# A decoder layer on one core: epsilon, the rotated sum and the last normalisation on GpSimd, the causal mask in quarters

## The chip, the cores and the metric

The kernel runs on one core of one Trainium2 chip. Its engines are TensorE (PE, with PEld for its weight loads), VectorE (DVE), ScalarE (ACT), GpSimd (POOL) and SyncE (SP, which only issues DMAs here). Each engine runs its own instructions in order and waits for semaphores that the others raise. The metric is the device time of one execution in microseconds (us), the median of several runs.

## What is computed

The reference is one decoder layer for 64 sequences of 64 rows with 256 features: rotary attention, a banded attention over context rows, a gated feed-forward layer with ternary weights, and a layer norm after each. Shortened:

```python
def _layernorm(x, g, b, eps=1e-05):
    mu = jnp.mean(x, axis=-1, keepdims=True)
    var = jnp.mean((x - mu) ** 2, axis=-1, keepdims=True)
    return (x - mu) * jax.lax.rsqrt(var + eps) * g + b
q = (_layernorm(x, qn_g, qn_b) @ Wq + bq)      # k, v likewise; 16 heads of 16
q = _rotary(q * scale, x)                      # a*fre - b*fim, a*fim + b*fre, by pairs
qn = _layernorm(q, ln_g, ln_b)                 # per head
scores = qn @ kn / sqrt(hd); scores = where(causal, scores, min)
out = softmax(scores) @ v @ Wo + bo
x = _layernorm(x + attn(x))
x = _layernorm(x + xattn(x, ctx))              # 8 heads of 8, |i - j| <= 64
# ffn: h = silu(gate) * up; hn = h * rsqrt(mean(h * h) + eps); hn @ w_proj
x = _layernorm(x + ffn(x))
```

## The kernel before

**Tiles and steps.** The 4096 rows are cut into 32 tiles of 128 rows (two sequences). The tiles run through a software pipeline that is written out by hand. Every engine has a function `step(at)`, called 41 times. In each step it does pieces of work of several tiles, and `at(-3)` is the tile that is three steps old. The order of the `put_...` calls inside `step` is the order on that engine. Nothing reorders it, so an instruction that waits holds up all that stands behind it. In the middle every step works on eight or nine tiles at different stages. The first six steps also hold the quantisation of the feed-forward weights (`quantise`, on DVE with ACT).

**Waits.** Each piece of work raises a semaphore of its own (`S["x2_lo"]` and so on). An instruction that reads what its own engine has just written waits for it too. On DVE `Chain` does that: it raises and waits after each instruction.

**The normalisations.** `put_x_stats`, `put_y1_stats`, `put_y2_stats` and `put_y3_stats` on DVE take mean and variance (`bn_stats`, `bn_aggr`) into `mv` and add epsilon into `base` (lines 1177, 1247, 1306, 1351). POOL raises `base` to the power -0.5 into `rstd` (`put_x_pow` and its like, lines 985, 1016, 1036, 1048), and DVE applies both. `put_yout` (line 1358, DVE) does so for the output, and `put_out` on SP stores it a step later. For the feed-forward layer ACT sums the squares (`put_sqsum`), DVE turns the sum into a mean plus epsilon (`put_hid_mean`, line 1332), POOL raises it to -0.5 (`put_hid_pow`, line 1044), ACT scales into `hsplit` (`put_h_hi`, line 842), and DVE computes the remainder in two halves (`put_h_lo`, line 1338). Behind `put_h_hi` ACT makes `headsT` (`put_ot`) and `attnT` (`put_aT`). PE transposes with line 559 what `put_h_hi` made, and its second group of line 492 waits for both `put_ot` and `put_aT`. The first group of line 492 stands ahead of line 559.

**Rotation.** POOL multiplies `qk` with sine and cosine into `rot2` and `rot1` (`put_rotated`, lines 993 and 994), the last work of its step. DVE adds the two (line 1201) and centres each head (lines 1202, 1203, `put_centred`). In the next step POOL goes on with `xbo` (line 1012), `x2_lo` (line 1040), `y3_pow` and the selects that cut the band (lines 1023, 1025). PE transposes `x2_hi` and `x2_lo` with line 518 and waits for `x2_lo` there.

**The mask.** `put_s_ps` on PE writes the causal mask (0 or -1e30, the same 64 rows twice) into two PSUM banks through an identity (line 360), two matmuls of 128 rows and 512 columns in bf16. On top of it the scores are summed with matmuls of 64 rows on the four quarters of the array (line 364).

Other lines: 430 the projections of the banded attention, 447 and 467 its scores for the maximum and for the exponential, 479 its values, 394 the values of the first attention (64 matmuls of 17 columns), 505 and 511 its output projections (511 waits for `gated` on POOL, line 1032), 1276 the row maxima, 1240 `y1`, 1187 `xn`, 1000 the powers of the head variances, 1007 `qkn`.

## Time and profile before

| | |
|---|---|
| runs | 1167.52, 1168.0, 1165.63 us, median 1167.52 |
| profiled execution | 1166.15 us, its span 1164.4 us |
| mean granted TensorE clock | 0.926 of full speed |
| busy in the span | PE 1050.6 us (90%), PEld 651.8 (56%), DVE 964.9 (83%), ACT 756.8 (65%), POOL 737.3 (63%) |
| chain that ended last | PE 73%, DVE 14%, POOL 4%, ACT 4%, issue 3%, DMA 1% |

A profile shows one execution. Busy time is the time in which an engine has an instruction in work; matmuls are pipelined, so a busy PE isn't PE at its peak. The chain follows the work that ended last back through what released it. In brackets behind an instruction stands how long its engine was idle before it, and whose signal ended that. PE's records are incomplete by a few per cent: line 360 has 33 rows for 64 matmuls.

### The profile page before, as it was taken

The numbers are of one execution on the slowest core, as the hardware profiler recorded it, in microseconds if no ns is written. First come the engines' busy times: TensorE is split into PE (matmuls) and PEld (weight loads), VectorE is DVE, ScalarE is ACT, GpSimd is POOL, SyncE is SP. The second block draws the span as 40 slices with busy tenths as digits, with TensorE's granted clock in tenths as the row PEclk, the third lists the DMA queues.
The fourth block names the chain that finished last, engine by engine and source line by source line (L and its number), as shares of the span: only waits on it lengthen the run. The fifth ranks groups of instructions, "written<-read, shape, count | busy, mean of one in ns | idle before, by whom it ended". The sixth has DMA issues, their size and how long they took to land.

```text
span 1164.4 us, 26192 instructions
## 1 busy us (share of the span) xinstructions
PE 1050.6 (90%) x10393; PEld 651.8 (56%) x10456; DVE 964.9 (83%) x2049; ACT 756.8 (65%) x1209; POOL 737.3 (63%) x1034
## 2 busy tenths in 40 slices
PE   4265899999999999999999999999999999999775
PEld 2143555666666666556655666666566556665442
DVE  5759778888898998998999899899989998887633
ACT  2343367677776777766777777777767777776652
POOL 1534477776677667767666677667767666664431
PEclk8656799999999999999999999999999999999877
DMA  6000000000000000000000000000000000000000
GB/s 213 10 5 10 16 15 16 16 11 11 20 21 20 21 20 20 21 20 21 2 19 21 20 21 20 21 20 21 21 20 21 3 19 20 17 16 11 10 20 9
DMA packets 26889, 25.04 MB, mean 22 GB/s; under 512 B 6160, under 2 KB 26000, under 8 KB 26768
## 3 DMA queue, kind: packets, MB, share of 16 engines
q1 hardware_dynamic: 24368, 20.23, 6.0%
q10 hardware_dynamic: 2400, 3.15, 0.8%
q8 instruction: 83, 1.36, 0.5%
q14 instruction: 38, 0.31, 0.1%
HBM read 14.19 MB, written 4.19 MB: 16 GB/s over the span
## 4 chain that ended last, share of the span: by engine, by line
PE 73%; DVE 14%; POOL 4%; ACT 4%; issue 3%; DMA 1%; SPq 0%; POOLq 0%; DVEq 0%
PE ps L430 10%; PE ps L479 8%; PE ps L394 6%; PE ps L333 5%; PE ps L548 5%; PE ps L565 5%; PE ps L532 5%; PE ps L447 4%; PE ps L467 4%; DVE hsplit L1338 3%; PE ps L340 3%; PE ps L364 3%; PE ps L378 2%; DVE rowmax L1276 2%; PE ps L511 2%
## 5 line engine op out<-in xcount | busy, mean ns | idle before, releaser
L1023 POOL TENSOR_SCALAR_AFFINE_SELECT prob<-prob 128x256 f32<-128x256 f32 (+1 forms) x256 | 137.5, 537 | 201.2 <-ACT prob L805 201.1
L1276 DVE TENSOR_REDUCE rowmax<-ps 128x4 f32<-128x768 f32 x256 | 243.2, 950 | 16.5 <-PE ps L447 15.7
L805 ACT ACTIVATE prob<-ps 128x768 f32<-128x768 f32 x256 | 207.0, 809 | 53.7 <-PE ps L467 53.3
L1000 POOL TENSOR_TENSOR hsum<-hsum,minus_half 128x8 f32<-128x8 f32 x128 | 210.7, 1687 | 36.6 <-DVE hsum L1211 33.4
L796 ACT ACTIVATE high<-ps,bx_col 128x512 f16<-128x512 f32 x128 | 99.6, 778 | 94.7 <-PE ps L430 91.9
L430 PE MATMUL ps<-x,wx_qk 128*128 128x256 f32 x512 | 139.9, 407 | 9.1 <-DVE k_rows L1264 4.4
L1025 POOL TENSOR_SCALAR_AFFINE_SELECT prob<-prob 128x512 f32<-128x512 f32 (+1 forms) x256 | 135.0, 527 | 0.0
L479 PE MATMUL ps<-prob,v_pad 128*32 128x192 f32 x2048 | 111.8, 336 | 1.0 <-POOL prob L1025 1.0
L430 PEld LDWEIGHTS ps<-x,wx_qk 128*128 128x128 f32 x512 | 93.0, 197 | 31.5 <-issue 13.7
L447 PE MATMUL ps<-k_rows,q_rows 24*128 24x192 f16 x1024 | 89.3, 254 | 4.0 <-DVE rowmax L1276 3.7
L467 PE MATMUL ps<-q_rows,k_rows 26*128 26x192 f16 x1024 | 88.2, 251 | 2.2 <-ACT prob L805 2.1
L1032 POOL TENSOR_TENSOR gated<-zr,enc 128x256 f32<-128x256 f32 x32 | 23.3, 729 | 97.1 <-ACT zr L819 97.1
L849 ACT ACTIVATE hT<-ps 128x1024 f16<-128x1024 f16 x64 | 65.6, 1025 | 19.3 <-PE ps L559 17.2
L394 PE MATMUL ps<-v_own,probT_a 64*64 64x17 f32 x1024 | 73.8, 212 | 4.1 <-ACT probT_a L781 4.1
L447 PEld LDWEIGHTS ps<-k_rows,q_rows 24*128 24x128 f16 x1024 | 29.1, 93 | 84.8 <-issue 69.8
L479 PEld LDWEIGHTS ps<-prob,v_pad 128*32 128x32 f32 x2048 | 53.9, 110 | 40.0 <-issue 16.9
L394 PE MATMUL ps<-v_swap,probT_a 64*64 64x17 f32 x1024 | 73.8, 212 | 2.1
L394 PEld LDWEIGHTS ps<-v_own,probT_a 64*64 64x64 f32 x1024 | 67.5, 140 | 9.3 <-issue 9.3
L394 PEld LDWEIGHTS ps<-v_swap,probT_a 64*64 64x64 f32 x1024 | 67.4, 140 | 5.3 <-PE ps L394 5.3
L333 PE MATMUL ps<-wqkv,xnT 128*128 128x512 f32 x128 | 67.8, 655 | 0.5 <-ACT xnT L757 0.5
L993 POOL TENSOR_TENSOR rot<-qk,sinT 128x256 f32<-128x256 f32 x64 | 46.1, 743 | 34.5 <-DVE qk L1191 34.5
L565 PE MATMUL ps<-wproj,hT 128*128 128x256 bf16 x512 | 66.2, 286 | 1.1 <-ACT hT L849 1.1
(147 smaller groups left out, 2440.7 us busy)
## 6 DMA issues: line engine op xcount, KB each, us to landing
v_swap<-v_own SPq DMA_DIRECT2D x64, 68.0 KB, 2.1
xin<-in_x SPq DMA_DIRECT2D x32, 128.0 KB, 2.1
enc<-in_ctx SPq DMA_DIRECT2D x32, 128.0 KB, 2.2
out<-yout SPq DMA_DIRECT2D x32, 128.0 KB, 2.0
prob<-in_w_gu ACTq DMA_DIRECT2D x4, 512.0 KB, 8.6
prob<-in_w_proj ACTq DMA_DIRECT2D x2, 512.0 KB, 13.0
q_rows<-negmax SPq DMA_DIRECT2D x64, 8.0 KB
q_rows<-in_Wkv SPq DMA_DIRECT2D x1, 512.0 KB, 7.8
```

The lines of the kernel that those rows point to most:

```text
L333: last = mm(ps[:, G6, :], xnT[:, i, :], wqkv[:, i, 0:512], start=i == 0, stop=i == 1)
L394: last = mm(ps[64 * b:64 * b + 64, G6, col:col + 17], probT_a[64 * half:64 * half + 64, slot // 2, 64 * b:64 * b + 64], vals[64 * half:64 ...
L430: last = mm(ps[:, (G7, G5, G5, G5)[c], XT * n:XT * n + XT], wx_qk[:, c, n, :], x1[:, t.x1_buf, :], start=True, stop=True)
L447: last = mm(ps[:, MXB + j, at:at + QW], q_rows[q, t.buf, ng, own], k_rows[q, t.buf, ng, others], start=True, stop=True)
L467: last = mm(ps[:, STB + j, at:at + QW], k_rows[q, t.buf, ng, own], q_rows[q, t.buf, ng, others], start=True, stop=True)
L479: last = mm(out[:, cols[kb]], v_pad[:, t.buf, kb, 4 * c + hq, :], prob[:, 4 * c + hq, kb, :], start=kb == 0, stop=kb == 1, skip_group_chec ...
L565: last = mm(ps[:, G6, 0:256], hT[:, i // 8, i % 8, :], wproj[:, i % 8, :], start=i == 0, stop=i == 15)
L805: copy(prob[:, 2 * c:2 * c + 2, :, :].rearrange("p u a b -> p u (a b)"), ps[:, STB:STB + 2, 0:2 * QW], ACT.Exp, scale=float(XD) ** -0.5).t ...
L1000: last = g.tensor_tensor(hsum[:, 1, h], hsum[:, 0, h], minus_half[:, h], ALU.pow)
L1023: g.affine_select(out=lead, in_=lead, compare_op=ALU.is_ge, fill=0.0, base=BAND - 64 * kb, pattern=[[0, 4], [1, cut]], channel_multiplier=-1)
L1025: last = g.affine_select(out=trail, in_=trail, compare_op=ALU.is_ge, fill=0.0, base=BAND + 64 * kb - cut, pattern=[[0, 4], [-1, QW - cut]] ...
L1276: v.tensor_reduce(of_head[:, hq:hq + 2, 2 * ng:2 * ng + 2], ps[:, MXB:MXB + 2, 0:2 * QW].rearrange("p j (a b) -> p j a b", a=2), AX, ALU.m ...
```

## The change

On POOL the four epsilon adds now stand right in front of the powers, each with a semaphore of its own that POOL waits for. The sum of squares gets its factor 1/1024 inside ACT's square (scale 1/32), and POOL adds epsilon to it, so that DVE's `put_hid_mean` is gone and `hid_pow` waits for `sqsum` on ACT. The add of the rotated parts moves from DVE to POOL, and `put_yout` moves from DVE to POOL, between the first two powers of the heads and `put_hid_pow`. The mask matmuls are four of 64 rows on the four quarters. `put_x_stats` signals after its last instruction. Everything else keeps its order.

```diff
@@ put_s_ps, PE
                 for r in range(2):
-                    mm(ps[:, G6 + r, :], identb[:, :], causal[:, :], start=True, stop=False, skip_group_check=True)
+                    q = slice(64 * r, 64 * r + 64)
+                    for b in range(2):
+                        mm(ps[64 * b:64 * b + 64, G6 + r, :], identb[q, q], causal[q, :], start=True, stop=False,
+                           skip_group_check=True, tile_position=(64 * r, 64 * b))
@@ put_sqsum, ACT
-                copy(sq_junk[:, :], hid[:, :], ACT.Square, accum_out=hss[:, 0:1]).then_inc(S["sqsum"], 1)
+                copy(sq_junk[:, :], hid[:, :], ACT.Square, scale=1.0 / 32, accum_out=hss[:, 0:1]).then_inc(S["sqsum"], 1)
@@ put_x_pow, POOL (put_y1_pow, put_y2_pow, put_y3_pow likewise)
                 pool.wait_ge(S["x_stats"], t.at(1, 1))
+                g.tensor_scalar(base[:, 0, :], mv[:, 0, 1:2], EPS, None, ALU.add).then_inc(S["eps0"], 1)
+                pool.wait_ge(S["eps0"], t.at(1, 1))
                 g.tensor_tensor(rstd[:, 0, :], base[:, 0, :], expo[:, :], ALU.pow).then_inc(S["x_pow"], 1)
@@ put_rotated, POOL
-                g.tensor_tensor(heads3(rot1[:, :]), heads3(qk[:, :]), cos_b, ALU.mult).then_inc(S["rotated"], 1)
+                g.tensor_tensor(heads3(rot1[:, :]), heads3(qk[:, :]), cos_b, ALU.mult).then_inc(S["rotated_c"], 1)
+                pool.wait_ge(S["rotated_c"], t.at(1, 1))
+                g.tensor_tensor(rot2[:, :], rot1[:, :], rot2[:, :], ALU.add).then_inc(S["rotated"], 1)
@@ put_hid_pow, put_yout, POOL
-                pool.wait_ge(S["hid_mean"], t.at(1, 1))
+                pool.wait_ge(S["sqsum"], t.at(1, 1))
+                g.tensor_scalar(hss[:, 2:3], hss[:, 0:1], 4 * RMS_EPS, None, ALU.add).then_inc(S["eps_hid"], 1)
+                pool.wait_ge(S["eps_hid"], t.at(1, 1))
                 g.tensor_tensor(hss[:, 3:4], hss[:, 2:3], expo[:, :], ALU.pow).then_inc(S["hid_pow"], 1)
...
+            def put_yout(t):
+                pool.wait_ge(S["y3_pow"], t.at(1, 1))
+                if t.has(3):
+                    pool.wait_ge(s_out[t.back(3).buf], t.back(3).dma(1))
+                g.tensor_scalar(yout[:, t.buf, :], y3[:, :], mv[:, 3, 0:1], rstd[:, 3, 0:1], ALU.subtract, ALU.mult).then_inc(S["yout"], 1)
@@ step, POOL
                     put_head_pow(t, 0)
                     put_head_pow(t, 1)
+                t = at(-8)
+                if t:
+                    put_yout(t)
                 t = at(-7)
                 if t:
                     put_hid_pow(t)
@@ put_x_stats, DVE
-                v.tensor_scalar(base[:, 0, :], mv[:, 0, 1:2], EPS, None, ALU.add).then_inc(S["x_stats"], 1)
                 chain(v.scalar_tensor_tensor(rot[:, 0:1], mv[:, 0, 0:1], mv[:, 0, 0:1], mv[:, 0, 1:2], ALU.mult, ALU.add))
-                chain(v.reciprocal(rot[:, 1:2], rot[:, 0:1]))
+                v.reciprocal(rot[:, 1:2], rot[:, 0:1]).then_inc(S["x_stats"], 1)
@@ put_centred, DVE
-                chain(v.tensor_tensor(rot2[:, :], rot1[:, :], rot2[:, :], ALU.add))
                 chain(v.tensor_reduce(hsum[:, 0, :], heads3(rot2[:, :]), AX, ALU.add))
@@ put_y1_stats, DVE (put_y2_stats, put_y3_stats likewise)
-                chain(v.bn_aggr(mv[:, 1, :], stat[:, 1, 0:6]))
-                v.tensor_scalar(base[:, 1, :], mv[:, 1, 1:2], EPS, None, ALU.add).then_inc(S["y1_stats"], 1)
+                v.bn_aggr(mv[:, 1, :], stat[:, 1, 0:6]).then_inc(S["y1_stats"], 1)
@@ put_hid_mean, put_yout, DVE: gone, with their calls
```

On POOL, at the end of one step and the start of the next, in the middle of the run, before:

```order
L1025 AFFINE_SELECT prob<-prob 128x4x64
L993 TENSOR_TENSOR rot<-qk,sinT 128x256 [waits c_qk]
L993 TENSOR_TENSOR rot<-qk,sinT 128x256
L994 TENSOR_TENSOR rot<-qk,cosT 128x512
L1012 TENSOR_TENSOR xbo<-xin,bo 128x256
L1040 TENSOR_TENSOR xsplit<-x,xsplit 128x256 [waits c_x2_hi]
L1048 TENSOR_TENSOR rstd<-base,expo 128x1 [waits c_y3_stats]
```

and after:

```order
L1034 AFFINE_SELECT prob<-prob 128x4x64
L998 TENSOR_TENSOR rot<-qk,sinT 128x256 [waits c_qk]
L998 TENSOR_TENSOR rot<-qk,sinT 128x256
L999 TENSOR_TENSOR rot<-qk,cosT 128x512
L1001 TENSOR_TENSOR rot<-rot 128x512 [waits c_rotated_c]
L1019 TENSOR_TENSOR xbo<-xin,bo 128x256
L1051 TENSOR_TENSOR xsplit<-x,xsplit 128x256 [waits c_x2_hi]
L1061 TENSOR_SCALAR base<-mv 128x1 [waits c_y3_stats]
L1063 TENSOR_TENSOR rstd<-base,expo 128x1 [waits c_eps3]
```

One instruction of 512 columns and a wait for POOL's own signal have come in between the product with `cosT` and `xbo`, and so ahead of `x2_lo`. An epsilon add has come in ahead of the power of `y3`.

On POOL, around the powers of the heads (`hsum<-hsum,minus_half`), before:

```order
L1000 TENSOR_TENSOR hsum<-hsum,minus_half 128x8 [waits c_variance]
L1000 TENSOR_TENSOR hsum<-hsum,minus_half 128x8
L1044 TENSOR_TENSOR hss<-hss,expo 128x1 [waits c_hid_mean]
L1000 TENSOR_TENSOR hsum<-hsum,minus_half 128x8 x2
L1007 TENSOR_TENSOR qkn<-rot,hsum 128x512 [waits c_head_pow3]
```

and after:

```order
L1007 TENSOR_TENSOR hsum<-hsum,minus_half 128x8 [waits c_variance]
L1007 TENSOR_TENSOR hsum<-hsum,minus_half 128x8
L1069 TENSOR_SCALAR yout<-y,mv,rstd 128x256 [waits s_out2,c_y3_pow]
L1055 TENSOR_SCALAR hss<-hss 128x1 [waits c_sqsum]
L1057 TENSOR_TENSOR hss<-hss,expo 128x1 [waits c_eps_hid]
L1007 TENSOR_TENSOR hsum<-hsum,minus_half 128x8 x2
L1014 TENSOR_TENSOR qkn<-rot,hsum 128x512 [waits c_head_pow3]
```

`yout` and the epsilon add have come in between the second power and `hid_pow` (`hss<-hss,expo`). `hid_pow` no longer waits for DVE's `hid_mean`; its epsilon add waits for ACT's `sqsum`.

On DVE, where the rotated parts are centred, before:

```order
L1269 TENSOR_TENSOR v_pad<-ps,bx_v 128x32x8 [waits c_vproj_ps]
L1201 TENSOR_TENSOR rot<-rot 128x512 [waits c_rotated]
L1202 TENSOR_REDUCE hsum<-rot 128x32 [waits c_centred_c]
L1203 SCALAR_TENSOR_TENSOR rot<-hsum,rot 128x512 [waits c_centred_c]
L1195 TENSOR_TENSOR v_own<-ps,qkv_bias 128x16x16 [waits c_v_ps]
```

and after:

```order
L1290 TENSOR_TENSOR v_pad<-ps,bx_v 128x32x8 [waits c_vproj_ps]
L1224 TENSOR_REDUCE hsum<-rot 128x32 [waits c_rotated]
L1225 SCALAR_TENSOR_TENSOR rot<-hsum,rot 128x512 [waits c_centred_c]
L1218 TENSOR_TENSOR v_own<-ps,qkv_bias 128x16x16 [waits c_v_ps]
L1339 SCALAR_TENSOR_TENSOR sg<-th,ps 128x512 [waits c_tanh0]
```

The add is gone, and the sum over each head waits for POOL's `rotated`, which now comes after POOL's add.

## Rows read from the trace of the kernel before

**Rows 1.** Table of stretches: length, busy us of PE, PEld, DVE, ACT, POOL, then granted clock.

```profile
500.00:600.00 100.00, 97.91 (x1025) 60.80 (x1034) 90.05 (x193) 70.72 (x114) 72.86 (x104) 0.98 0.06 18
292.60:296.00 3.40, 3.40 (x31) 2.21 (x30) 1.64 (x3) 2.13 (x3) 3.40 (x3) 0.50 0.31 97
961.60:965.00 3.40, 3.40 (x25) 2.85 (x22) 2.23 (x5) 2.08 (x4) 3.32 (x3) 0.50 0.44 123
39.60:163.40 123.80, 86.83 (x643) 54.98 (x646) 90.05 (x160) 52.26 (x80) 55.90 (x58) 0.68 0.03 9
```

**Rows 2.** Timeline of DVE, three steps: start us, us, engine, line, operation, tiles.

```profile
927.12 0.40 DVE L1187 TENSOR_SCALAR xn<-xin,mv,rstd 128x256 f32<-128x256 f32 x1
...
958.63 0.41 DVE L1187 TENSOR_SCALAR xn<-xin,mv,rstd 128x256 f32<-128x256 f32 x1
...
991.02 0.40 DVE L1187 TENSOR_SCALAR xn<-xin,mv,rstd 128x256 f32<-128x256 f32 x1
```

**Rows 3.** Chain of waits, one step at the mask: start us, us, what.

```profile
499.92 0.65 PE ps L430 x3
...
500.62 0.38 PE ps L360
501.00 1.02 PE ps L364 x16
```

**Rows 4.** Timeline of POOL and PE at `x2_lo` and line 518.

```profile
182.51 0.68 POOL L1040 TENSOR_TENSOR xsplit<-x,xsplit 128x256 f16<-128x256 f32 x1
...
183.95 0.40 PE L518 MATMUL ps<-ident,xsplit 128*128 128x128 f16 x4
...
498.64 0.42 POOL L1023 TENSOR_SCALAR_AFFINE_SELECT prob<-prob 128x256 f32<-128x256 f32 x1 [3.21 <-ACT prob L805]
...
1012.36 0.67 POOL L1040 TENSOR_TENSOR xsplit<-x,xsplit 128x256 f16<-128x256 f32 x1
...
1013.80 0.40 PE L518 MATMUL ps<-ident,xsplit 128*128 128x128 f16 x4
...
1141.25 0.67 POOL L1040 TENSOR_TENSOR xsplit<-x,xsplit 128x256 f16<-128x256 f32 x1 [2.02 <-ACT xsplit L823]
...
1141.98 0.40 PE L518 MATMUL ps<-ident,xsplit 128*128 128x128 f16 x4 [2.03 <-POOL xsplit L1040]
```

**Rows 5.** Groups of instructions by shape: count | busy us, mean ns | idle us before.

```profile
L1023 POOL TENSOR_SCALAR_AFFINE_SELECT prob<-prob 128x256 f32<-128x256 f32 x128 | 53.5, 418 | 201.2 <-ACT prob L805 201.1
...
L994 POOL TENSOR_TENSOR rot<-qk,cosT 128x512 f32<-128x512 f32 x32 | 40.9, 1278 | 0.0
...
L1007 POOL TENSOR_TENSOR qkn<-rot,hsum 128x512 f32<-128x512 f32 x32 | 36.3, 1136 | 2.5
...
L1012 POOL TENSOR_TENSOR xbo<-xin,bo 128x256 f32<-128x256 f32 x32 | 23.3, 729 | 0.0
...
L1201 DVE TENSOR_TENSOR rot<-rot 128x512 f32<-128x512 f32 x32 | 21.8, 682 | 0.1
...
L980 POOL MEMSET expo<- 128x1 f32 x1 | 0.1, 99 | 0.0
```

**Rows 6.** Timeline of all engines from `hid_pow` to line 505.

```profile
515.97 0.56 POOL L1044 TENSOR_TENSOR hss<-hss,expo 128x1 f32<-128x1 f32 x1
...
516.56 1.15 ACT L842 ACTIVATE hsplit<-hid,hss 128x1024 f16<-128x1024 f32 x1 [1.30 <-POOL hss L1044]
...
518.52 0.66 PE L492 MATMUL ps<-ident,headsT 128*128 128x128 f32 x4
...
518.79 0.74 DVE L1338 SCALAR_TENSOR_TENSOR hsplit<-hid,hss,hsplit 128x512 f16<-128x512 f32 x1
...
519.82 1.06 POOL L1007 TENSOR_TENSOR qkn<-rot,hsum 128x512 f32<-128x512 f32 x1
...
520.00 1.42 DVE L1338 SCALAR_TENSOR_TENSOR hsplit<-hid,hss,hsplit 128x512 f16<-128x512 f32 x1
...
521.82 0.48 PE L505 MATMUL ps<-heads_f,wx_out 128*128 128x256 f32 x1 [0.44 <-DVE y L1240]
```

48 lines of the change are left out of this document (19 added, 29 removed).

## Prediction

> **What bounds the kernel now.** I read three views in turn: the table of stretches, the chain of waits, and the timeline of single steps on each engine. In 100 us of the middle PE is busy for 97.9, DVE for 90.1, POOL for 72.9 and ACT for 70.7 us [rows 1]. A middle step takes 31.51 us (the `xn` instructions at 927.12 and 958.63), some take 32.39 (958.63 to 991.02) [rows 2]. The granted clock explains the longer ones: from 961.60 to 965.00 it was 0.50 of full speed, the 1.2 GHz level instead of 2.4, just after the step's 64 short matmuls of line 394. There are eight such falls between 290 and 1010 us, the first at 292.60 and the last at 961.60 [rows 1].
>
> The chain is PE from one step to the next [rows 3]. It leaves PE only for a stretch of DVE that ends with `y` (line 1240), and for the handover through `zr` and `gated`. So two things matter: how long PE's own work is, and how much slack the other engines have where PE picks up their results. A spare microsecond on DVE buys little. A microsecond on POOL costs nothing while it is smaller than the slack behind it.
>
> **Part A: the rotated parts are added on POOL.** DVE loses the add of line 1201 (682 ns [rows 5]), and POOL gets it behind the product with `cosT`. Behind that stand `xbo` and `x2_lo` (line 1040), and PE's transposes of line 518 wait for `x2_lo`. POOL can't begin this passage earlier, since the selects ahead of it wait for an `exp` (3.21 us of idle time) that follows PE. In step 7 `x2_lo` ends at 182.51 + 0.68 = 183.19 and PE takes it up at 183.95. In step 33 it ends at 1013.03 and PE takes it up at 1013.80 [rows 4]. The distance is 0.76 us in all 27 steps between, because PE comes straight from other matmuls. With nothing in the way the handover takes 0.06 us (1141.25 + 0.67 against 1141.98 [rows 4]), so the slack is 0.62 to 0.70 us; I take 0.68.
>
> The trace has no add of two dense 512-column operands on POOL. Line 994 with two operands of that length takes 1278 ns. Line 1007, whose second operand is one value for sixteen columns, takes 1.06 us undisturbed. Two dense 256-column operands take 729 ns, so twice that, 1.46, is the upper end [rows 5, 6]. I take 1.28, the row with the same reads per element. The add also waits for its predecessor's signal, which costs 0.08 us (line 1007's idle time: 2.5 us in 32 cases [rows 5]). So the passage grows by 1.36 us and PE's transposes come 1.36 - 0.68 = 0.68 us late. PE has no idle time between there and the value matmuls to win it back. **27 x 0.68 = +18.4 us**, with the ends 27 x (1.14 - 0.70) = +11.9 and 27 x (1.54 - 0.62) = +24.8. The Trainium skill (GPSIMD Engine Reference, section 4.1 "Engine selection") speaks against this part: two-input elementwise work is about twice as slow on GpSimd as on VectorE. By that the add would take 1.36 us and the term would be 20.6 us; the 1278 ns row agrees closely.
>
> **Part B: `yout` goes in front of `hid_pow` on POOL.** POOL comes to `hid_pow` at 515.97 without a pause, straight from two powers of 8 columns. ACT waits for it (1.30 us idle) and then makes `h_hi`, `headsT` and `attnT` one after the other. PE's second group of line 492 waits for these last two and starts at 518.52 without a pause [rows 6]. Now `yout` and an epsilon add with its own wait come between. `yout` reads one stream of 256 columns. A select of that size takes 418 ns and a two-stream instruction 729; I take 0.45, nearest to the select, which also reads one stream. The epsilon add has one column: a memset of one column takes 99 ns, the power of one column 0.56 us. I take 0.20, nearer to the memset, since nothing is raised to a power [rows 5, 6]. With the 0.08 wait `hid_pow` comes about 0.70 us later (0.5 to 1.3). The mean that DVE made (line 1332) goes away with its handover, which gains nothing, as POOL was busy with the powers beyond it.
>
> The second group of line 492 then comes 0.70 us late in a usual step. PE had 0.44 us of room later, where line 505 waited for `y` until 521.82 [rows 6], so 0.26 us is left if `y` comes on time. `y` stands behind the second half of line 1338, which took 1.42 us at 520.00 where the first half took 0.74 at 518.79. The long one started 0.18 us after `qkn` on POOL at 519.82 [rows 6]. The Trainium skill (SBUF — State Buffer, section "Who interferes with whom") has the reason: a DVE instruction with two SBUF inputs and a GpSimd instruction that reads SBUF exclude each other, whichever starts first. The 1.42 against 0.74 agrees. After the change both start 0.5 to 0.7 us later, within 0.02 us of each other by my sums. DVE first leaves 0.26 us a step, POOL first about twice that, 0.53. I take 0.4. In steps with a fall of the clock PE comes there so late that the delay is hidden, which leaves 16 steps: **16 x 0.4 = +6.4 us**, with the ends 0 and 16 x 1.1 = +17.6.
>
> **Part C: the mask in quarters.** The two matmuls of 512 columns lie on the chain from 500.57 (499.92 + 0.65, the end of line 430) to 501.00, 0.43 us a step. Four quarters that run at once would take 0.21 us, four in turn 0.86. The sixteen pieces of line 364, which stand on the same four quarters, take 1.02 us together [rows 3]. That is 0.06 each for 256 columns, less than half of the mask's 0.21 for 512, so they overlap; I take 0.21. But the saving lies between the start of POOL's passage and line 518, so PE just reaches its new wait earlier. Only the six steps without that passage keep it: **6 x -0.21 = -1.3 us** (+2.6 if they run in turn, since +0.43 hides under the 0.68 elsewhere).
>
> **Part D: the rest.** DVE is relieved by 0.68 us, by `yout` and by five one-column instructions, together somewhat under 2 us a step. In the middle hardly anybody waits for that. In the first steps (39.60 to 163.40: DVE busy 90 and PE 87 of 124 us [rows 1]) I count 1 us a step over four steps, half of it on the path: **-2 us** (-4 to +2, since the add is also slower on POOL and meets the weight quantisation). The other epsilon adds on POOL come before idle time, such as the 3.21 us above: nothing. `x_stats` now signals after the reciprocal, while POOL is busy elsewhere: nothing. `put_out` on SP waits for `yout` one step later: nothing. In the last tiles `yout` and the epsilon adds are bare: **+0.7 us**. A fall of the clock costs 32.39 - 31.51 = 0.88 us. The new waits of PE stand near the short matmuls, so I expect three falls more: **+2.6 us** (-7 if all go, +16 if every step has one).
>
> **Sum.** 18.4 + 6.4 - 1.3 - 2 + 0.7 + 2.6 = +24.8 us on the profiled execution's 1166.15 us gives 1190.9. The median of the runs is 1.4 us above that execution, so 1192 us, 2.1% slower.
>
> **The rivals.** Rival 1, faster. POOL's additions fit into the slack and only the relief counts: 32 x -0.21 for the mask, -2 in the first steps, +0.7 at the end give 1159.5 us. For it speaks that POOL is idle for 27% of the middle. Against it, the idle time lies before the selects and not in this passage. It decides at an add of 0.60 us, against 1.06 in the shortest row. If only A fits and B doesn't, it is 1166.
>
> Rival 2, the clock. PE now pauses twice a step near its low-activity matmuls, and the clock falls in nearly every step: 13.4 us more, 1205. For it: the falls already follow line 394. Against it: two steps of three have none, though PE pauses for 0.44 us there. The Trainium skill (TensorE: Matmul & The Clock Gate, section "A second HAM failure mode: psum-queue depth-cycling") tells of a kernel whose short pauses between groups made the clock swing. Whether pauses of 0.7 us do so, no row here shows.
>
> Rival 3, the upper ends of part B. `yout` costs 0.73, the epsilon add 0.56, and `qkn` is first at the port: 17.6 instead of 6.4 us, 1203.
>
> Rival 4, the small delay. The add takes 1.06, DVE comes first, a few falls go: 11.9 + 1.5 - 2.6 - 4 us, 1174.
>
> **How the numbers follow.** Forecast 60% (own range 1180 to 1202), rival 1 10%, rival 2 14%, rival 3 8%, rival 4 8%. About 0.2% (2.3 us) is what a measurement can tell from no change. Faster by more: 7%, out of rival 1. Within it: 7%, the mixed form of rival 1 and half of rival 4 with more falls gone. Slower: 86%. The range of 1172 to 1207 us leaves out rival 1, the lowest part of rival 4 and what lies above rival 2.
>
> **What would show it.** Right: the transposes now wait for `x2_lo`, about 0.7 us in 27 steps; POOL's add takes near 1.28; ACT's idle time before `h_hi` grows from 1.30 to about 2.0; a step without a fall grows from 31.5 to about 32.5; POOL is busy for 79% of the middle; the mask block shrinks by 0.2 and the step doesn't. Wrong: no wait before the transposes (part A falls), a fall in more than half of the steps (rival 2), or a second half of line 1338 at 0.74 in every step, which leaves part B at 0.26.

## The result, and the profile after

The changed kernel takes 1233.7 us (median; 1230.9 to 1236.1), the kernel before beside it 1166.6 us (1163.6 to 1168.0). The ratio is 1.0578 with a 95% interval of 1.0544 to 1.0612: 5.8% slower, where 2.1% was forecast, and above the range's upper end of 1207 us. The profiled execution took 1230.9 us, with a span of 1229.2 us and a mean granted clock of 0.893 (0.926 before).

From the page of the changed kernel, the busy time and the chain that ended last:

```profile
PE 1082.9 (88%) x10488; PEld 667.2 (54%) x10520; DVE 932.8 (76%) x1825; ACT 755.0 (61%) x1209; POOL 870.7 (71%) x1258
...
PE 48%; POOL 27%; DVE 10%; ACT 9%; issue 3%; DMA 1%; SPq 0%; POOLq 0%; DVEq 0%
```

POOL's share of the chain was 4% and is 27%. Line numbers have moved: 360, 394, 430, 505, 518, 559 are now 362, 397, 433, 508, 521, 562; 842 is 845, 1007 is 1014, 1040 is 1051, 1044 is 1057, 1338 is 1354. New on POOL are line 1001 (the rotated add), 1055 (epsilon for `hid`) and 1069 (`yout`).

The table of stretches of the changed kernel, with the columns of [rows 1]: first the middle, then one long and one short fall of the clock:

```profile
500.00:600.00 100.00, 95.01 (x965) 58.56 (x966) 81.09 (x162) 66.08 (x108) 79.08 (x115) 0.93 0.06 18
608.93:615.76 6.83, 6.43 (x42) 4.38 (x32) 4.10 (x10) 3.74 (x5) 5.59 (x6) 0.50 0.28 83
711.33:714.74 3.41, 3.39 (x30) 2.02 (x23) 1.83 (x5) 1.63 (x3) 3.25 (x5) 0.50 0.39 116
```

In 100 us PE is busy 3 us less than before, and POOL is busy for 79. Before, a fall to the 1.2 GHz level lasted 3.4 us each time, and there were 8 between 290 and 1010 us (27.2 us in all). Now there are 20 in that stretch, 98.6 us in all. Nine of them last 6.83 us, a length that the trace of before does not show there. (All sums of falls here count a short one as 3.4 us and a long one as 6.8.)

The timeline of POOL, ACT and PE in a usual step, one with a short fall (start, duration, engine, line, operation, tiles; in brackets the idle time before and who ended it):

```profile
810.02 3.31 POOL L1007 TENSOR_TENSOR hsum<-hsum,minus_half 128x8 f32<-128x8 f32 x2
813.33 1.24 POOL L1069 TENSOR_SCALAR yout<-y,mv,rstd 128x256 f32<-128x256 f32 x1
814.65 0.23 POOL L1055 TENSOR_SCALAR hss<-hss 128x1 f32<-128x1 f32 x1
814.96 0.57 POOL L1057 TENSOR_TENSOR hss<-hss,expo 128x1 f32<-128x1 f32 x1
815.57 1.15 ACT L845 ACTIVATE hsplit<-hid,hss 128x1024 f16<-128x1024 f32 x1 [2.94 <-POOL hss L1057]
816.86 0.73 PE L562 MATMUL ps<-ident,hsplit 128*128 128x128 f16 x8
```

The same place in the only step between 290 and 1010 us without a fall:

```profile
679.86 1.15 ACT L845 ACTIVATE hsplit<-hid,hss 128x1024 f16<-128x1024 f32 x1 [2.94 <-POOL hss L1057]
681.15 0.61 PE L562 MATMUL ps<-ident,hsplit 128*128 128x128 f16 x8 [1.35 <-ACT hsplit L845]
683.07 0.74 DVE L1354 SCALAR_TENSOR_TENSOR hsplit<-hid,hss,hsplit 128x512 f16<-128x512 f32 x1
683.36 1.37 POOL L1014 TENSOR_TENSOR qkn<-rot,hsum 128x512 f32<-128x512 f32 x1
```

And the same transposes in the kernel before, in the step of [rows 6]:

```profile
517.96 0.61 PE L559 MATMUL ps<-ident,hsplit 128*128 128x128 f16 x8
```

`yout` takes 1.24 us, not 0.45. `hid_pow` comes 1.6 us after the powers instead of directly behind them [rows 6]. ACT's idle time ahead of `h_hi` has grown from 1.30 to 2.94 us. And PE, which came to `h`'s transposes without a pause before, now waits 1.35 us in front of them in the step without a fall. In the steps with a fall PE is slowed on its way there, so that less of that wait is left: 0.07 us or none in those with a short fall, up to 0.47 in those with a long one.

The groups of the changed kernel by shape, as in [rows 5]:

```profile
L1001 POOL TENSOR_TENSOR rot<-rot 128x512 f32<-128x512 f32 x32 | 42.8, 1338 | 2.5
...
L1069 POOL TENSOR_SCALAR yout<-y,mv,rstd 128x256 f32<-128x256 f32 x32 | 39.6, 1238 | 0.3
...
L988 POOL TENSOR_SCALAR base<-mv 128x1 f32<-128x1 f32 x32 | 18.6, 582 | 14.3 <-DVE rot L1202 14.3
...
L1055 POOL TENSOR_SCALAR hss<-hss 128x1 f32<-128x1 f32 x32 | 7.2, 226 | 11.7 <-ACT sq_junk L841 9.6
```

The group of line 521, where PE takes up `x2_lo` ([rows 4] showed it without a wait):

```profile
L521 PE MATMUL ps<-ident,xsplit 128*128 128x128 f16 x128 | 12.6, 221 | 26.6 <-POOL xsplit L1051 26.6
```

**The steps.** The `xn` instructions of the changed kernel, timeline of DVE, as in [rows 2]:

```profile
641.18 0.40 DVE L1210 TENSOR_SCALAR xn<-xin,mv,rstd 128x256 f32<-128x256 f32 x1
...
675.72 0.40 DVE L1210 TENSOR_SCALAR xn<-xin,mv,rstd 128x256 f32<-128x256 f32 x1
...
708.97 0.40 DVE L1210 TENSOR_SCALAR xn<-xin,mv,rstd 128x256 f32<-128x256 f32 x1
...
742.77 0.40 DVE L1210 TENSOR_SCALAR xn<-xin,mv,rstd 128x256 f32<-128x256 f32 x1
```

The three steps between them take 34.54 us (with a long fall at 643.07), 33.25 (none) and 33.80 (a short one at 711.33). So a step without a fall has grown from 31.51 to 33.25, by 1.74 us (the changed kernel has only this one; the filled form below has six of the same length). The mean of the middle steps has grown from 31.82 to 34.18, by 2.36. The difference of 0.62 a step comes in the steps with a fall. Over 27 steps that is 47 us of waiting and 17 us with the falls, which together nearly account for the 67. This is a reckoning by step lengths: in a step with a fall, part of the waiting lies hidden under PE's slower work. Nor is all of the 0.62 us shown to be the clock's, as the run with `yout` back on DVE shows.

### The profile page after: what moved, and what is told of

Its sections match the earlier page's. It is cut to its first block, busy times and chain, and to the rows that moved or that the text cites. A ratio compares the mean times of both kernels' runs of the same rounds, so it can differ in the third digit from the quotient of the medians.

```text
span 1229.2 us, 26319 instructions
## 1 busy us (share of the span) xinstructions
PE 1082.9 (88%) x10488; PEld 667.2 (54%) x10520; DVE 932.8 (76%) x1825; ACT 755.0 (61%) x1209; POOL 870.7 (71%) x1258
## 3 DMA queue, kind: packets, MB, share of 16 engines
q8 instruction: 84, 1.38, 0.5%
## 4 chain that ended last, share of the span: by engine, by line
PE 48%; POOL 27%; DVE 10%; ACT 9%; issue 3%; DMA 1%; SPq 0%; POOLq 0%; DVEq 0%
PE ps L433 5%; PE ps L568 5%; POOL hsum L1007 4%; PE ps L535 4%; POOL prob L1032 4%; PE ps L482 3%; POOL rot L998 3%; PE ps L397 3%; POOL prob L1034 3%; POOL rot L1001 3%; POOL rot L999 3%; PE ps L551 3%; PE ps L450 3%; PE ps L340 3%; ACT prob L808 3%
## 5 line engine op out<-in xcount | busy, mean ns | idle before, releaser
L1007 POOL TENSOR_TENSOR hsum<-hsum,minus_half 128x8 f32<-128x8 f32 x128 | 213.6, 1687 | 25.5 <-DVE hsum L1233 25.5
L482 PE MATMUL ps<-prob,v_pad 128*32 128x192 f32 x2048 | 121.1, 358 | 1.0 <-POOL prob L1034 0.9
L450 PE MATMUL ps<-k_rows,q_rows 24*128 24x192 f16 x1024 | 92.2, 261 | 2.9 <-DVE rowmax L1297 2.8
L845 ACT ACTIVATE hsplit<-hid,hss 128x1024 f16<-128x1024 f32 x32 | 36.7, 1148 | 82.6 <-POOL hss L1057 82.6
L852 ACT ACTIVATE hT<-ps 128x1024 f16<-128x1024 f16 x64 | 65.5, 1024 | 12.7 <-PE ps L562 12.1
L1354 DVE SCALAR_TENSOR_TENSOR hsplit<-hid,hss,hsplit 128x512 f16<-128x512 f32 x64 | 64.0, 1002 | 8.2 <-ACT hsplit L845 8.1
```

The costliest lines, as they stand in the source:

```text
L450: last = mm(ps[:, MXB + j, at:at + QW], q_rows[q, t.buf, ng, own], k_rows[q, t.buf, ng, others], start=True, stop=True)
L482: last = mm(out[:, cols[kb]], v_pad[:, t.buf, kb, 4 * c + hq, :], prob[:, 4 * c + hq, kb, :], start=kb == 0, stop=kb == 1, skip_group_chec ...
L1007: last = g.tensor_tensor(hsum[:, 1, h], hsum[:, 0, h], minus_half[:, h], ALU.pow)
```

## The experiments

Two theories stood at the start. P, the price: each operation moved costs what its wait takes out of PE's step, and nothing else. C, the clock: PE's new pauses bring falls of the clock, and these cost more than the wait does. The falls are counted between 290 and 1010 us. A "clean" step is the usual length of the shortest steps without a fall, read as above from the `xn` instructions; in the changed kernel it is a single step. "Mean" is the mean of the 21 middle steps. Steps and falls come from one profiled execution a kernel, and that can lie away from the median: the add alone was profiled at 1195.8 us (median 1189.1), the first filled kernel at 1186.3 (1193.2). Each ratio is to the kernel before on the same chip.

### Each part undone or done alone

**`yout` back on DVE**, the rest as changed.

```diff
 POOL step
-                    put_yout(t)
 DVE step, ahead of put_max(t, 0), as before
+                    put_yout(t)
```

> The changed kernel with put_yout back on DVE, everything else as changed. Theory P (price): the whole delay behind hid_pow comes from yout's 1.24 us on GpSimd. A middle step went from 31.51 to 33.80 us, of which 1.6 us lie between the powers of the heads and line 508 (now). Without yout the epsilon add leaves hid_pow about 0.35 us late, which PE's 0.44 us of room hides. So 26 steps times 1.6 = 42 us come back: about 1192 us. Theory C (clock): the loss is kept up by the falls of the granted clock, one in nearly every step now, which any wait of PE brings on, line 521's too. Then they stay when yout goes, and the time is 1205 us or more.

1188.5 us, ratio 1.0202 (1.0136 to 1.0267); clean step 32.00, mean 32.68, 13 falls (44.2 us), all short. The number is theory P's. Of the 45 us that came back, 27 x 1.25 = 34 are waiting by the clean steps, and the rest went with the falls. Three steps in a row of this kernel tell apart two things that come together in the changed one, a short fall and a long second half of `h_lo` (line 1345 here):

```profile
653.79 0.40 DVE L1201 TENSOR_SCALAR xn<-xin,mv,rstd 128x256 f32<-128x256 f32 x1
...
659.90 1.64 DVE L1345 SCALAR_TENSOR_TENSOR hsplit<-hid,hss,hsplit 128x512 f16<-128x512 f32 x1
...
686.34 0.40 DVE L1201 TENSOR_SCALAR xn<-xin,mv,rstd 128x256 f32<-128x256 f32 x1
...
693.47 0.74 DVE L1345 SCALAR_TENSOR_TENSOR hsplit<-hid,hss,hsplit 128x512 f16<-128x512 f32 x1
...
719.36 0.41 DVE L1201 TENSOR_SCALAR xn<-xin,mv,rstd 128x256 f32<-128x256 f32 x1
```

The first takes 32.55 us, with the long `h_lo` and no fall (granted clock 1.00). The second takes 33.02, with a short `h_lo` and a short fall. The next, with neither, takes 32.00. So a long `h_lo` costs 0.55 us by itself here, as much as the steps of 33.80 us in the changed kernel stand above its 33.25.

**The add back on DVE**, the rest as changed.

```diff
 put_rotated, POOL
-                g.tensor_tensor(rot2[:, :], rot1[:, :], rot2[:, :], ALU.add)
 put_centred, DVE
+                chain(v.tensor_tensor(rot2[:, :], rot1[:, :], rot2[:, :], ALU.add))
```

> The changed kernel with the add of the rotated parts back on DVE, everything else as changed. Theory P: PE's wait before the transposes of x2 (line 521) goes away, 27 steps times 0.72 us = 19 us, and part of the mask's 0.21 us a step appears, about 5 us: 1210 us; GpSimd's wait at hid_pow stays as it is. Theory C: with one of the two waits gone the falls of the clock go back to one step in three, which is worth 10 us or so more: 1200 us.

1222.6 us, ratio 1.0492 (1.0435 to 1.0549). Both expectations missed by far, since the wait at `x2_lo` was gone and almost nothing came back. `xn` on DVE in this kernel, and two stretches of the table:

```profile
597.43 0.41 DVE L1208 TENSOR_SCALAR xn<-xin,mv,rstd 128x256 f32<-128x256 f32 x1
...
631.57 0.41 DVE L1208 TENSOR_SCALAR xn<-xin,mv,rstd 128x256 f32<-128x256 f32 x1
...
665.70 0.41 DVE L1208 TENSOR_SCALAR xn<-xin,mv,rstd 128x256 f32<-128x256 f32 x1
```

```profile
634.53:641.36 6.83, 6.28 (x36) 4.48 (x32) 4.27 (x10) 3.74 (x5) 5.65 (x6) 0.50 0.26 79
668.66:675.49 6.83, 6.28 (x36) 4.48 (x32) 4.27 (x11) 3.74 (x5) 5.66 (x6) 0.50 0.27 79
```

Every middle step takes 34.13 us, with one 6.83 us fall at the same place in each (21 falls, 142.8 us). The steps have fallen into time with the falls. What is left of the change here is `yout`, epsilon and the mask.

**The mask alone**, on the kernel before.

```diff
-                    mm(ps[:, G6 + r, :], identb[:, :], causal[:, :], start=True, stop=False, ...)
+                    (four quarters, as in the change)
```

> The kernel before with the mask in quarters alone. Theory P: PE is the bound there and the block gets 0.21 us shorter in each of 32 steps: 1166.6 - 6.7 = 1160 us. Rival: PE meets another wait (x2_lo with 0.7 us of slack isn't one, but y before line 505 is in two steps of three, so that the time would come back there) and the time stays at 1166 us within 2 us.

1159.9 us, ratio 0.9962 (0.9931 to 0.9993). The clean step is 31.29 instead of 31.51, 0.22 less; 9 falls.

**`yout` alone on POOL**, on the kernel before (in front of `hid_pow`, as in the change).

```diff
 POOL step
+                    put_yout(t)
                     put_hid_pow(t)
 DVE step
-                    put_yout(t)
```

> The kernel before with put_yout alone moved to GpSimd, in front of hid_pow as in the change. It makes hid_pow about 1.25 us late. Price alone: PE's 0.44 us of room takes some, 26 steps of 0.9 us, 23 us: 1188 us. Theory C (the clock locks on): the step then is 32.4 to 32.8 us long by its waits, and the run with the add on DVE again showed that a step of about 33 us is stretched to 34.13 us with a fall of 6.8 us in every one of them. If the same happens here, 26 steps of 2.3 to 2.6 us: 1220 to 1228 us.

1178.9 us, ratio 1.0110 (1.0078 to 1.0141); clean step 32.18, mean 32.49, 12 falls, all short. Less than either expected. Of the 1.24 us only 0.67 stay in the clean step: the second half of `h_lo` now takes 0.74 us and PE no longer waits for `y` at line 505.

**The add alone on POOL**, on the kernel before.

```diff
 put_rotated, POOL
+                g.tensor_tensor(rot2[:, :], rot1[:, :], rot2[:, :], ALU.add)
 put_centred, DVE
-                chain(v.tensor_tensor(rot2[:, :], rot1[:, :], rot2[:, :], ALU.add))
```

> The kernel before with one edit: the addition of the rotated parts moved from DVE to GpSimd; final normalisation, epsilon additions and mask stay as before. Price theory P: the addition takes 1.27 us on GpSimd and TensorE's transposes at line 518 come 0.72 us later in each of 27 steps, +19 us, so 1186 us (1183 to 1190), with falls of the clock in about 10 steps of 22. Clock theory C: a step that waits is stretched until one fall of the clock comes in each of them, as in the changed kernel; then the mean middle step is 33.5 or more and the time 1205 or more.

1189.1 us, ratio 1.0215 (1.0184 to 1.0246); clean step 32.13 (+0.62), mean 32.71, 13 falls, all short. Slightly above theory P, far below C. 27 x 0.62 = 17 us is the wait, and the rest comes with five more falls.

**Epsilon alone**: the changed kernel with `yout` and the add back on DVE, so that the mask in quarters and the epsilon adds are left.

```diff
 POOL
-                    put_yout(t)
-                g.tensor_tensor(rot2[:, :], rot1[:, :], rot2[:, :], ALU.add)
 DVE
+                    put_yout(t)
+                chain(v.tensor_tensor(rot2[:, :], rot1[:, :], rot2[:, :], ALU.add))
```

> The changed kernel with both moved operations back on DVE: the addition of the rotated parts and the final normalisation. What is left of the change is the mask in quarters and the two epsilon additions on GpSimd (0.22 us each, one of them behind hid_out and ahead of hid_pow). If the epsilon additions cost what they measure on the path, hid_pow is 0.25 us late in 27 steps, some of it regained before line 505: 1160 + up to 6, so 1160 to 1166. If they cost nothing (the old bias operand that they replace cost the same), 1160, as the mask alone. If any delay of this place is stretched by the clock, 1172 or more.

1164.6 us, ratio 1.0008 (0.9986 to 1.0030). Against the mask alone (0.9962) the epsilon adds cost about 5 us, as expected, though the two intervals overlap.

### The place or the engine

**`yout` on POOL, but ahead of the fourth select**, the rest as changed.

```diff
 POOL step
+                    put_yout(t)
                     put_sel(t, 3)
 ...
-                    put_yout(t)
                     put_hid_pow(t)
```

> The changed kernel with put_yout still on GpSimd but earlier in its step, behind the power of x and ahead of the fourth select, where GpSimd was idle for 1.44 us. Theory of place: what counts is that yout stood in front of hid_pow, not that it is on GpSimd. Its 1.24 us fit into the idle time, and the time is that of the run with yout on DVE: 1188 to 1191 us. Rival: GpSimd is simply overloaded, the delay moves to the fourth select and with it to the powers of the heads, and the time stays above 1215 us.

1191.4 us, ratio 1.0216 (1.0182 to 1.0250), the same as with `yout` on DVE (1.0202). The instruction still costs 1.24 us of POOL, but here POOL would be idle. So it is the place that costs. One fall of this kernel is long, the other eight are short.

**The same with the add back on DVE.**

```diff
 put_rotated, POOL
-                g.tensor_tensor(rot2[:, :], rot1[:, :], rot2[:, :], ALU.add)
 put_centred, DVE
+                chain(v.tensor_tensor(rot2[:, :], rot1[:, :], rot2[:, :], ALU.add))
```

> The changed kernel with the final normalisation on GpSimd ahead of the fourth selection instead of ahead of hid_pow, and the addition of the rotated parts back on DVE. If place decides and not the engine, nothing of the path carries either operation: 1160 to 1167 us, the mask alone with up to 6 for the epsilon addition. If the normalisation ahead of the selection makes the selection late, probT at line 397 waits for it: 1.24 us less GpSimd's idle time there, up to 27 times 0.5, 1173 or more.

1166.0 us, ratio 1.0006 (0.9988 to 1.0025). It is equal to before and to the kernel with both on DVE (1.0008). That POOL can carry `yout` free of charge is shown; a gain from relieving DVE is not to be had.

**The price of such an instruction.** Eight unused instructions ran once in one step of the kernel before. Six of them are shown, each one line of the following view (one line of the program, its count, min/median/max ns):

```diff
+                if at.number == 20:
+                    g.tensor_scalar(junk[:, 0, :], src, pc, pd, ALU.subtract, ALU.mult)
+                    g.tensor_scalar(junk[:, 1, :], src, 0.5, 2.0, ALU.subtract, ALU.mult)
+                    g.tensor_scalar(junk[:, 2, :], src, pc, None, ALU.mult)
+                    g.tensor_scalar(junk[:, 3, :], src, 2.0, None, ALU.mult)
+                    g.tensor_copy(junk[:, 4, :], src)
+                    g.tensor_tensor(junk[:, 5, :], src, bo[:, :], ALU.add)
```

> The kernel before with eight more instructions on GpSimd, once, in step 20, ahead of the fourth select of a step, where it is idle. They write to a tile of their own. They price the form of yout: 256 columns with subtract and multiply by two per-partition operands; the same with two constants; one per-partition operand; one constant; a copy; an add of two tiles; the first form on 128 columns; an epsilon add on one column. Theory P1: the per-partition operands cost it (1.24 us with them, about 0.45 with constants). Theory P2: the number of operations costs it (1.24 for both forms with two operations, 0.45 to 0.7 with one). Theory P3: tensor_scalar is slow in any form (1.2 us in all four) and only the copy takes 0.4.

```profile
L1071 POOL TENSOR_SCALAR junk<-qkv_bias,lncol x1: 1328/1328/1328, 598.9 to 598.9; 128x256 f32<-128x256 f32 x1
L1072 POOL TENSOR_SCALAR junk<-qkv_bias x1: 1188/1188/1188, 600.3 to 600.3; 128x256 f32<-128x256 f32 x1
L1073 POOL TENSOR_SCALAR junk<-qkv_bias,lncol x1: 926/926/926, 601.5 to 601.5; 128x256 f32<-128x256 f32 x1
L1074 POOL TENSOR_SCALAR junk<-qkv_bias x1: 843/843/843, 602.4 to 602.4; 128x256 f32<-128x256 f32 x1
L1075 POOL COPY junk<-qkv_bias x1: 391/391/391, 603.2 to 603.2; 128x256 f32<-128x256 f32 x1
L1076 POOL TENSOR_TENSOR junk<-qkv_bias,bo x1: 718/718/718, 603.5 to 603.5; 128x256 f32<-128x256 f32 x1
```

All have 256 columns in f32. A copy takes 0.39 us and an add of two tiles 0.72. The instruction with a scalar takes 0.84 with one operation and 1.19 with two, although it reads one stream only. Operands that come from a column of memory add 0.08 to 0.14. So the number of operations decides most of it (theory P2), though one operation costs more than P2 expected. Each price is one reading.

### The clock

**Unused matmuls in the pause.** The kernel with the add back on DVE (1222.6 us above) got two matmuls of 512 columns ahead of PE's wait for `h_hi`. Their result is never read.

```diff
 put_hT_ps, PE
+                    pe.wait_ge(S["hid0"], t.at(1, 1))
+                    for i in range(2):
+                        mm(ps[:, G5, :], xsplitT[:, i, :], wgu[:, i, 0:512], start=True, stop=True)
                     pe.wait_ge(S["h_hi"], t.at(1, 1))
```

> The changed kernel with the add on DVE again (1222.6 us, every middle step 34.13 us with a fall of the clock of 6.8 us), and two more matmuls of 512 columns in front of PE's wait for h_hi, whose result is overwritten and not used. Theory C: PE's pause there keeps the clock low for the second half of the fall. With the pause filled the falls get shorter (3.4 us) or rarer and the time goes down although work was added, to about 1200 us. Theory P: the clock follows the small matmuls of line 397 and the pause has no part in it. Then the added work, 0.43 us a matmul at the low clock against 0.55 us of idle time, costs 0.3 us a step or nothing: 1222 to 1232 us.

1193.2 us, ratio 1.0210 (1.0173 to 1.0248): 29 us less by the medians, 33 by the ratios, with more work. The falls went from 21 (142.8 us) to 13 (44.2 us) and all are short; the clean step is 32.39, the mean 32.79.

**The same two matmuls in the changed kernel itself.**

> The changed kernel with two unused matmuls of 512 columns put into TensorE's program just ahead of its wait for h_hi, in a bank that is free there; they lie in the pause and their result is never read. Clock theory C: the pause of TensorE in front of line 562 brings the fall of the clock in every step; with it filled, falls drop from 20 to 13 or fewer of 22 middle steps, and the time from 1234 to 1205 to 1217. Price theory P: the added waits alone make the 1234 us; the filling takes nothing away, 1234 to 1245.

1213.3 us, ratio 1.0414 (1.0387 to 1.0441): 20 us less. Here too no fall is longer than 3.4 us (15 falls, 51.0 us). The clean step stays at 33.24, and the long `h_lo` comes about as often (12 of 22 steps against 13 of 21), so the matmuls took no waiting away: the 20 us are the clock's.

### Which part is `yout`'s partner

The parts alone add up to a ratio of 1.033 (-0.0038 for the mask, +0.0110 `yout`, +0.0215 the add, +0.0046 epsilon), and the change measured 1.058. `yout` alone had short falls only, and with mask and epsilon beside it a long one in each step. Two partners were possible. M: the mask in quarters, since it leaves PE less work. L: the epsilon add, since it makes PE's pause longer.

**`yout` and the mask**, no epsilon, no add.

```diff
 the kernel with yout alone on POOL
-                    mm(ps[:, G6 + r, :], identb[:, :], causal[:, :], start=True, stop=False, ...)
+                    (four quarters, as in the change)
```

> The kernel before with the final normalisation on GpSimd ahead of hid_pow and the mask in quarters; epsilon and the addition of the rotated parts as before. Theory M (the mask in quarters is the partner, since its block has PE at less work before the pause): a fall of 6.8 us in nearly every middle step, steps near 34.1, 1215 us or more. Theory L (the length of PE's pause before line 562 is what decides, and the epsilon addition is the partner): as the normalisation alone less the mask's gain, 1179 - 4 = 1175 us (1171 to 1180), falls of 3.4 us.

1178.4 us, ratio 1.0097 (1.0067 to 1.0127); clean 31.99, mean 32.33, 11 falls.

**`yout` and epsilon**, whole mask, no add.

```diff
 the changed kernel with the add back on DVE
-                    (four quarters, as in the change)
+                    mm(ps[:, G6 + r, :], identb[:, :], causal[:, :], start=True, stop=False, ...)
```

> The changed kernel without the mask in quarters and with the addition of the rotated parts on DVE: the final normalisation and the epsilon additions on GpSimd are left. Theory M: as the normalisation alone plus the epsilon, 1179 + 5 = 1184 us (1180 to 1190). Theory L: the later hid_pow makes PE's pause about 1 us and brings a 6.8 us fall in nearly every step, 1215 us or more.

1220.9 us, ratio 1.0470 (1.0440 to 1.0499); clean 32.78, mean 34.03, 19 falls (105.4 us), twelve of them long.

**The changed kernel with the whole mask.**

```diff
 put_s_ps, PE
-                    (four quarters, as in the change)
+                    mm(ps[:, G6 + r, :], identb[:, :], causal[:, :], start=True, stop=False, ...)
```

> The changed kernel with the mask in two whole matmuls as before, all else as changed. Theory M: the interaction goes and the time falls to 1200 to 1212 us, falls of 3.4 us only. Theory L: it stays, 1230 to 1240 us.

1230.5 us, ratio 1.0542 (1.0520 to 1.0564); clean 33.27, mean 34.14, 20 falls (95.2 us), eight of them long. The mask in quarters gains nothing in this kernel.

**`yout` and a pure delay**: the kernel before, with `yout` on POOL and an unused copy between it and `hid_pow`.

```diff
                     put_yout(t)
+                    g.tensor_copy(junk[:, :], bo[:, :])
                     put_hid_pow(t)
```

> The kernel before with the final normalisation on GpSimd ahead of hid_pow, and between the two an unused copy of 256 columns on GpSimd (0.39 us, its result is never read): a pure delay of hid_pow, as large as that of the epsilon addition, with the whole mask. Theory L: 6.8 us falls in nearly every step, 1215 us or more. Theory M: 1179 + 27 x 0.4 = up to 1190 us.

1219.5 us, ratio 1.0438 (1.0383 to 1.0493); clean 32.54, mean 33.68, 19 falls (102.0 us), eleven of them long. A copy of 0.40 us costs about 38 us (1.0110 to 1.0438). Theory L holds in all four by the times, and M in none; but long falls come in about half of the steps, not in nearly every one. The copy and the pause of PE behind it, timeline of this kernel:

```profile
834.49 1.23 POOL L1055 TENSOR_SCALAR yout<-y,mv,rstd 128x256 f32<-128x256 f32 x1
835.67 0.40 POOL L1084 COPY junk<-bo 128x256 f32<-128x256 f32 x1
836.03 0.57 POOL L1045 TENSOR_TENSOR hss<-hss,expo 128x1 f32<-128x1 f32 x1
...
837.92 0.61 PE L560 MATMUL ps<-ident,hsplit 128*128 128x128 f16 x8 [1.32 <-ACT hsplit L843]
```

The same place with `yout` alone:

```profile
652.41 0.61 PE L559 MATMUL ps<-ident,hsplit 128*128 128x128 f16 x8 [0.96 <-ACT hsplit L842]
```

**The changed kernel without epsilon** (on DVE as before; mask, `yout` and add as changed).

```diff
 put_hid_pow, POOL (the four other powers likewise)
-                g.tensor_scalar(hss[:, 2:3], hss[:, 0:1], 4 * RMS_EPS, None, ALU.add)
 put_hid_mean, DVE
+                v.tensor_scalar(hss[:, 2:3], hss[:, 0:1], 1.0 / HID, 4 * RMS_EPS, ALU.mult, ALU.add)
```

> The changed kernel with the epsilon additions (and the mean of the squares of hid) on DVE as before; mask in quarters, normalisation and addition of the rotated parts on GpSimd. Theory L (the length of PE's pause before the transposes of h decides): parts add up, 1166 + 23.5 + 12 - 4.5 = 1197 us (1193 to 1206), falls mostly of 3.4 us. Rival (any two pauses in one step bring a long fall in each): 1225 us or more, falls of 6.8 us.

1203.2 us, ratio 1.0333 (1.0271 to 1.0395); clean 32.80, mean 33.17, 9 falls (37.4 us), two of them long. That is the 1.033 to which the parts add up; two pauses in a step do not by themselves bring the long falls. The pause in this kernel:

```profile
663.79 0.61 PE L562 MATMUL ps<-ident,hsplit 128*128 128x128 f16 x8 [0.90 <-ACT hsplit L845]
```

The kernels side by side, the pause read in a step without a fall:

| kernel | pause before `h`'s transposes | clean step | mean - clean | falls, us | long ones |
|---|---|---|---|---|---|
| before | none | 31.51 | 0.31 | 8, 27.2 | 0 |
| the add alone | none | 32.13 | 0.58 | 13, 44.2 | 0 |
| change, `yout` on DVE | none | 32.00 | 0.68 | 13, 44.2 | 0 |
| `yout` alone | 0.96 | 32.18 | 0.31 | 12, 40.8 | 0 |
| `yout` and mask | 0.93 | 31.99 | 0.34 | 11, 37.4 | 0 |
| change without epsilon | 0.90 | 32.80 | 0.37 | 9, 37.4 | 2 |
| the change, filled | 0.82 | 33.24 | 0.33 | 15, 51.0 | 0 |
| `yout` + copy | 1.32 | 32.54 | 1.14 | 19, 102.0 | 11 |
| the change | 1.35 | 33.25 | 0.93 | 20, 98.6 | 9 |
| the change, whole mask | 1.35 | 33.27 | 0.87 | 20, 95.2 | 8 |
| `yout` and epsilon | 1.38 | 32.78 | 1.25 | 19, 105.4 | 12 |

The clean steps of the add and of `yout` add up: 31.51 + 0.62 + 0.67 = 32.80, as measured without epsilon. Epsilon's part doesn't: it is 0.45 between that kernel and the change, and 0.60 between `yout` alone and `yout` with epsilon. The table shows that pauses of 1.3 us and more go with 8 to 12 long falls, and those up to 0.96 us with two at most (the kernels with both moved operations out of this place have two as well). The length of the step isn't what decides: the change and its filled form have the same clean step. The surcharge of mean over clean follows this pause only in part. The add, whose pause of 0.66 us lies elsewhere, before line 518, brings it from 0.31 to 0.58 with short falls alone.

**For a better kernel**: the mask in quarters and the second half of `h_lo` ahead of `heads` on DVE, both on the kernel before.

```diff
+                    put_h_lo(t, 1)
                     put_heads(t, 1)
-                    put_h_lo(t, 1)
```

> The kernel before with the mask in quarters (1159.9 us alone) and, on DVE, the second half of h_lo in front of the second half of heads. So it starts about 0.55 us earlier and ahead of qkn on GpSimd, and takes 0.74 instead of 1.4 us. Theory of the port: y comes up to 0.6 us earlier and PE's 0.4 us wait before line 508 goes in two steps of three: 16 steps of 0.3 to 0.4 us, 1154 us. Rival: heads now comes 0.66 us later and PE waits for it instead, before its transposes: 1160 us or more.

1161.8 us, ratio 0.9957 (0.9932 to 0.9981), against 0.9962 for the mask alone. The order on DVE gains nothing: PE waits for the later `heads` instead of `y`. The mask alone, or this, is the best version found, 0.4% faster than before.

## Why the prediction was wrong

**What bounds the kernel** was read rightly: a delay on POOL costs nothing up to the slack behind it, and the rest goes into PE's step one for one. Two findings bear it out. The kernel with `yout` ahead of the select pays nothing for it (1.0216 with it on POOL against 1.0202 with it on DVE). And the clean steps of the add and of `yout` add up.

**Part A was right.** The add takes 1.27 us in the usual step (1.28 taken), the mean of 1338 ns lies a little above. PE waits for `x2_lo` in 28 steps, 26.6 us in all, some 0.9 a step. That is the delay and the 0.2 us by which the shorter mask brings PE there earlier. Alone, the part makes the clean step 0.62 us longer against the 0.68 of the sum. Its 25 us instead of 18.4 are 17 of waiting and the rest falls.

**Part B failed, and its term was mis-sized.** The step that failed is "`yout` reads one stream of 256 columns ... I take 0.45, nearest to the select". It takes 1.24 us, above the upper bound of 0.729. The number of streams was the wrong measure. The probe shows that the scalar instruction takes 0.84 us with one operation and 1.19 with two, at the same single stream. No row of before had that instruction on POOL, so both bounds came from other kinds of instruction. The epsilon add was right (0.20 taken, 0.23 measured). So `hid_pow` came 1.6 us late instead of 0.70. (The prediction's own terms, 0.45 + 0.20 + 0.08, make 0.73, and its upper ones 1.37 where it says 1.3; that changes nothing.) Rival 3 had doubted the right term, but with 0.73 us for `yout` it stopped at 1203. PE meets the delay one group earlier than computed, at the transposes of `h_hi` and not at the second group of line 492. There it had little slack: before, `h_hi` ended at 516.56 + 1.15 = 517.71, and PE took it up at 517.96. The room of 0.44 us at line 505 was there, and in the clean steps 0.57 us were won back, since the second half of `h_lo` went down to 0.74: part B leaves 0.67 + 0.45 = 1.12 us a clean step, against 0.26 to 0.53. The race of `h_lo` and `qkn` was foreseen as a toss-up and is one: row 683.07 shows 0.74 us with `qkn` 0.29 behind it, others 1.64 with `qkn` 0.04 behind it, and with `yout` on DVE both 1.64 and 0.74 occur with `qkn` 0.04 behind. In the changed kernel the steps of 33.80 are those with the long `h_lo`, and there PE waits for `y` at line 508 again.

**Part C was right.** The mask saves 0.22 us a step where nothing waits (31.29 against 31.51 when alone). In the changed kernel it saves nothing that shows: 1.0578 with it, 1.0542 without it.

**Part D failed at the clock.** "I expect three falls more: +2.6 us". There were twelve more between 290 and 1010 us, and most of the added low-clock time came from falls of twice the old length. With 0.62 us a step that comes to 17 us. Filling the pause gave 20 us back. The bound of +16 "if every step has one" was reached. What the step had wrong is the size and the kind: it priced falls at 0.88 us each, all of the old length. Rival 2 had named the mechanism, a fall in nearly every step, but for pauses of 0.7 us. There it is borne out only in part: the add alone brings 13 short falls in 21 steps and about 7 us. The long falls in number came only because part B's pause was twice as long as computed. The epsilon additions, counted at nothing or at 0.2 us of waiting, became the last straw: 5 us alone, 29 us here (1.0333 to 1.0578), of which 27 x 0.45 = 12 are waiting by the clean steps. The relief of DVE in the first steps (-2) can't be told apart from nothing: both kernels that keep some of it stand at 1.0006 and 1.0008.

**The signs given.** POOL's 79% came true, but by a longer `yout` in longer steps. The add's price, the wait at line 521 and the mask came true. ACT's idle time (2.0 expected, 2.94 measured) and the clean step (32.5 against 33.25) pointed to part B, and a fall in more than half of the steps to rival 2. With the measured prices the same sum gives 27 x 0.62 + 27 x 1.12 = 47 us of waiting before any clock. The forecast's 25 could not have been mended by the clock alone.

The Trainium skill (TensorE: Matmul & The Clock Gate, section "A second HAM failure mode: psum-queue depth-cycling") had pointed to short pauses between groups of matmuls. This case agrees for pauses of 1.3 us in this place (19 and 20 falls, most of the added time in long ones) and weakly for those of 0.7 to 1.0 us (9 to 15 falls, against 8 in the kernel before, nearly all short).

**What stays open.** Why the kernel with mask, `yout` and epsilon but no add falls into the even beat of 34.13 us, and pays more to the clock (34.13 against a clean 32.39, read from its filled form) than the full change does, was not settled. That the beat of the steps and that of the falls lock together is seen in its rows; why just there was not tried. In the steps of 33.80 us a short fall and the long `h_lo` come together. The 0.55 us that a long `h_lo` costs by itself with `yout` on DVE could be all that they stand above 33.25. So the step lengths don't settle how much of the 17 us is the clock's; the 20 us that filling gave back came as the long falls went. And the pause in a step at full clock marks a kernel, not each fall: with the copy, long falls stand in steps where PE pauses for 0.25 us (from 697.0 us on), and with `yout` and mask a short one where it pauses for 0.54 (from 515.5 on). Where in the step a fall begins seems to count as well; this was not tried.

## What to carry to other kernels

Read the price of an instruction on an engine from a row with the same kind of instruction and the same number of operations there. If the trace has none, measure it, or widen the range a good deal (here 0.45 was taken and 1.24 measured). A delay in front of PE has two prices: the wait, which adds up from part to part and can be read off the steps at full clock, and the clock, which shows little for a short pause (some 7 us for the add's) and came as a jump for one somewhat longer. So sum the delays that end in the same pause before judging any of them, and where a pause can't be avoided, try to fill it. Work for a half-idle POOL belongs in front of its idle time, not in a passage for which others wait.

## What the hardware showed that was not expected

- A scalar instruction on POOL costs by its number of operations: 843 ns for one, 1188 for two constants, on 256 f32 columns where a copy takes 391 and a two-tile add 718.
- 0.4 us more of pause ahead of PE's transposes made 19 falls of 12 short ones, 11 of them of 6.8 us, and cost about 38 us in 1179. Unused matmuls there gave 29 and 20 us back.
- A kernel's steps can lock to the falls: 34.13 us each, with a 6.83 us fall at the same place in each of them.
- A one-column add on POOL takes 0.22 to 0.23 us in four places. In the fifth it takes 0.58 on average (line 988, 0.64 in the middle steps), next to DVE's two-input instruction of line 1225; that this neighbour is the cause was not tried.
